# Two buffers for the attention's output weight, and the last query tile's output products moved into the next group's order

## The reference

```python
x = x + 0.5 * _L0_ffn_ref(_layernorm(x), ...)      # attention and a mixture of experts
x = x + _L0_attn_ref(_layernorm(x), ...)           # a recurrent-style token mix
x = x + 0.5 * _L0_ffn_ref(_layernorm(x), ...)      # the first part again, same weights
```

```python
q = (x @ wq).reshape(b, s, H, HD); k = (x @ wk)...; v = (x @ wv)...
q = apply_rope(q, cos, sin); k = apply_rope(k, cos, sin)
scores = jnp.einsum('bqhd,bkhd->bhqk', q, k) / np.sqrt(HD)
probs = jax.nn.softmax(jnp.where(causal, scores, min), axis=-1)
out = jnp.einsum('bhqk,bkhd->bqhd', probs, v).reshape(b, s, H * HD)
return out @ wo
```

## Time and profile before

| | |
|---|---|
| median of three runs | 1355.61 us |
| lowest and highest run | 1352.35 and 1356.25 us |
| the profiled execution, its own time | 1357.88 us |
| its span from first to last instruction | 1356.1 us |
| PE busy | 1174.1 us (87%) |
| DVE busy | 955.6 us (70%) |
| ACT busy | 773.1 us (57%) |
| POOL busy | 599.1 us (44%) |
| mean granted TensorE clock | 0.925 of full |
| chain that ended last, share by engine | PE 80%, DVE 11%, ACT 3%, DMA 2%, POOL 2% |

### The profile page before, as it was taken

The page is one execution under the profiler, slowest core; times in us unless marked ns, Lnnn a source line. Parts: engine busy times, 40 slices in busy tenths (PEclk is TensorE's granted clock), DMA queues, the critical chain, the costliest instruction groups (busy, mean ns, idle before and its releaser), DMA issues.

```text
span 1356.1 us, 18606 instructions
## 1 busy us (share of the span) xinstructions
PE 1174.1 (87%) x6576; PEld 976.2 (72%) x6576; DVE 955.6 (70%) x1799; ACT 773.1 (57%) x1510; POOL 599.1 (44%) x450
## 2 busy tenths in 40 slices
PE   5799999999999499963398799999999999849994
PEld 4688788788787378851277578878878878638883
DVE  6677677777787757748757667777777778757774
ACT  5666566666564167742453656656666656417772
POOL 3664575575610034521412375466476370004541
PEclk9899999999999589995789799999999989859998
DMA  4100100100000941124100200010010000193113
GB/s 126 36 0 2 35 1 1 35 1 1 1 1 1 318 159 51 51 81 144 51 1 1 66 1 1 1 36 1 1 36 1 1 1 1 40 347 103 51 52 117
DMA packets 48651, 66.29 MB, mean 49 GB/s; under 512 B 5808, under 2 KB 34352, under 8 KB 48432
## 3 DMA queue, kind: packets, MB, share of 16 engines
q1 hardware_dynamic: 42032, 50.94, 11.5%
q0 software_dynamic: 4416, 12.06, 2.9%
q10 hardware_dynamic: 2112, 2.10, 0.4%
HBM read 54.86 MB, written 10.22 MB: 48 GB/s over the span
## 4 chain that ended last, share of the span: by engine, by line
PE 80%; DVE 11%; ACT 3%; DMA 2%; POOL 2%; issue 2%; SPq 0%; DVEq 0%; POOLq 0%; ACTq 0%
PE ps L1375 21%; PE ps L1377 19%; PE ps L1376 19%; PE ps L1444 9%; PE ps L1505 6%; PE ps L1493 2%; PE ps L1432 1%; POOL probs L681 1%; DVE h L1079 1%; DMA xs<-rows_dram,token_of 1%; PE ps L1513 1%; PE ps L1476 1%; PE ps L1347 1%; DVE negmax L1058 1%; DVE mixT L1309 1%
## 5 line engine op out<-in xcount | busy, mean ns | idle before, releaser
L748 ACT ACTIVATE probs<-ps,negmax 128x128 f32<-128x128 f32 (+7 forms) x256 | 189.6, 741 | 109.2 <-DVE negmax L1058 106.9
L754 ACT ACTIVATE probsT<-ps 128x512 fp32r<-128x512 f32 x288 | 168.6, 597 | 135.6 <-PE ps L1444 133.4
L1058 DVE TENSOR_REDUCE negmax<-ps 128x1 f32<-128x128 f32 (+7 forms) x256 | 191.2, 751 | 64.0 <-PE ps L1432 62.0
L1063 DVE TENSOR_TENSOR probsT<-ps,probsT 128x512 fp32r<-128x512 f32 x288 | 195.0, 686 | 44.7 <-ACT probsT L754 42.8
L1444 PE MATMUL ps<-square,probs 128*128 128x128 f32 x1152 | 170.1, 275 | 5.9 <-DVE values L1053 5.9
L652 POOL DMA_INDIRECT xs<-rows_dram,token_of x46 | 68.5, 1489 | 214.3 <-DVE token_of L1154 181.8
L608 POOL TENSOR_TENSOR crossed<-crossed,rope 128x512 f32<-128x512 f32 x70 | 91.5, 1308 | 161.3 <-ACT crossed L735 161.3
L1079 DVE SCALAR_TENSOR_TENSOR h<-ps,rowinv,h 128x256 f32<-128x256 f32 x256 | 123.2, 481 | 48.5 <-PE ps L1377 36.1
L1444 PEld LDWEIGHTS ps<-square,probs 128*128 128x128 f32 x1152 | 134.1, 141 | 25.7 <-DVE values L1053 6.2
L1375 PE MATMUL ps<-keysT,queriesT 128*128 128x512 f32 (+3 forms) x384 | 141.2, 368 | 9.1 <-ACT probs L748 4.3
L1162 DVE TENSOR_TENSOR parts<-experts,parts 128x1024 fp32r<-128x1024 f32 x92 | 112.2, 1225 | 49.7 <-ACT parts L794 49.2
(11 more groups left out here) (229 smaller groups left out, 2897.7 us busy)
## 6 DMA issues: line engine op xcount, KB each, us to landing
experts<-in_L_ffn_w_dram SPq DMA_DIRECT2D x48, 512.0 KB, 10.5
w_in<-in_L_ffn_wq_dram SPq DMA_DIRECT2D x8, 512.0 KB, 3.9
wo_in<-in_L_ffn_wo_dram SPq DMA_DIRECT2D x8, 512.0 KB, 6.3
rows_dram<-probs ACTq DMA_DIRECT2D x4, 512.0 KB, 10.1
probs<-y_dram SPq DMA_DIRECT2D x8, 256.0 KB, 4.2
mixT<-y_dram SPq DMA_DIRECT2D x8, 256.0 KB, 4.7
probs<-in_L_attn_x_dram SPq DMA_DIRECT2D x2, 512.0 KB, 4.5
w_in<-in_L_ffn_wk_dram SPq DMA_DIRECT2D x8, 128.0 KB, 4.7
```

The costliest lines, as they stand in the source:

```text
L748: act.activation(probs[:, i % 2, k, 0:w], ps[:, 2 * slot_n:2 * slot_n + 2, :].rearrange("p b n -> p (b n)")[:, 0:w], ACT.Exp, bias=negmax[ ...
L754: act.activation(probsT[:, m % 3, 0, :], ps[:, 4 + m % 2, :], ACT.Copy).then_inc(S["probsT_high"], 1)
L1058: dve.tensor_reduce(negmax[:, m:m + 1], ps[:, s:s + 2, :].rearrange("p b n -> p (b n)")[:, 0:w], AX.X, ALU.max, negate=True).then_inc(S["m ...
L1063: dve.tensor_tensor(probsT[:, m % 3, 1, :], ps[:, 4 + m % 2, :], probsT[:, m % 3, 0, :].bitcast(F32), ALU.subtract).then_inc(S["probsT_low ...
```

## The change

The buffer `w_o` becomes a pair, used by even and odd groups. The second one takes the place in memory of `w_v`, the split value weight, which is needed only while the values of a call are computed. POOL now splits the next group's output weight at the end of a group's own list without waiting for that group's `out` steps: it waits for the group before it (or, in the first group, for the last value product).

The four kinds of step that project a tile out (`attn_high`, `attn_low`, `out`, `added`) go into a helper, `project_out`. A group that has a successor no longer calls it for its tile 7. The successor's order calls it for a tile -1, before anything else, and plans it among its own first steps. Two limits come with it: `values` 1,0, which needs the PSUM bank, comes after `added` -1,1, and so does `max` 3,0.

```diff
+    def project_out(i):
+        add("ACT", ("attn_high", i, 0), 0.52, i + 1.2, ("values", i, i), ("attn_high", i - 1, 0), ("out", i - 2, 1))
+        add("DVE", ("attn_low", i, 0), 0.75, i + 1.2, ("attn_high", i, 0), ("attn_low", i - 1, 0))
+        for k in range(2):
+            add("PE", ("out", i, k), 0.64, i + 1.3 + 0.2 * k, ("attn_low", i, 0), ("added", i, k - 1), ("out", i - 1, 1),
+                ("wo_split", 0, 0))
+            add("DVE", ("added", i, k), 0.95 if more or not k else 1.4, i + 1.3 + 0.2 * k, ("out", i, k), ("added", i, k - 1), ("added", i - 1, 1))
+    if carry:
+        project_out(-1)
+        later += [(("values", i, 0), ("added", -1, 1)) for i in (1,)] + [(("max", 3, 0), ("added", -1, 1))]
...
+        if i < NT - 1 or not more:
+            project_out(i)
...
+            w_o = [sb("w_o_even", [P, 2, REP, D], F32R, c=phase), None]
+            with ExitStack() as opening_phase:
+                w_v = sb("w_v", [P, 2, DC, KVH * HD], F32R, c=opening_phase)
+            w_o[1] = sb("w_o_odd", [P, 2, REP, D], F32R, c=phase)
...
-        ORDERS = {more: group_order(more)[0] for more in (True, False)}
+        ORDERS = {more: group_order(more, carry=True)[0] for more in (True, False)}
...
-                    pool.wait_ge(S["out_ps"], 2 * NT * (grp.gg + 1))
-                    split(grp.gg + 1, w_o, wo_in[:], "wo_in", 16, "wo_split")
+                    if g:
+                        pool.wait_ge(S["out_ps"], 2 * NT * grp.gg)
+                    else:
+                        pool.wait_ge(S["v_done_ps"], NT * (f + 1))
+                    split(grp.gg + 1, w_o[(grp.gg + 1) % 2], wo_in[:], "wo_in", 16, "wo_split")
...
-                        if k == 0:
-                            if i >= 2:
-                                pe.wait_ge(S["out_added"], REP * (NT * gg + i - 1))
+                        if k == 0 and (g or i >= 2):
+                            pe.wait_ge(S["out_added"], REP * (NT * gg + i - 1))
...
-                                            parts(w_o, hd, every), True, True)
+                                            parts(w_o[(gg - (i < 0)) % 2], hd, every), True, True)
```

More of the change, by code:

```diff
@@ L51, in turns_before, with group_order @@
     return i * (i + 1) // 2
-def group_order(more, opening=False):
+def group_order(more, opening=False, carry=False):
     steps = {}
@@ L99, in group_order @@
             add("PE", ("values", i, j), 0.64, at + 1.0 / (i + 1), ("low", i, j), ("values", *last), ("added", i - 2, 1))
-        add("ACT", ("attn_high", i, 0), 0.52, i + 1.2, ("values", i, i), ("attn_high", i - 1, 0), ("out", i - 2, 1))
-        add("DVE", ("attn_low", i, 0), 0.75, i + 1.2, ("attn_high", i, 0), ("attn_low", i - 1, 0))
-        for k in range(2):
-            add("PE", ("out", i, k), 0.64, i + 1.3 + 0.2 * k, ("attn_low", i, 0), ("added", i, k - 1), ("out", i - 1, 1),
-                ("wo_split", 0, 0))
-            add("DVE", ("added", i, k), 0.95 if more or not k else 1.4, i + 1.3 + 0.2 * k, ("out", i, k), ("added", i, k - 1), ("added", i - 1, 1))
+        if i < NT - 1 or not more:
+            project_out(i)
     for n, (w, k, at) in enumerate(blocks):
@@ L701, in rwkv @@
                 first_weights(1)
-                split(KVH, w_o, wo_in[:], "wo_in", 16, "wo_split")
+                split(KVH, w_o[0], wo_in[:], "wo_in", 16, "wo_split")
             attention(0)
@@ L1078, in group @@
                                 dve.wait_ge(S["out_added"], REP * (NT * gg + i) + hd)
-                            dve.scalar_tensor_tensor(out=h[:, i, :], in0=ps[:, 6 + i % 2, (hd % 2) * D:(hd % 2 + 1) * D],
-                                                     scalar=rowinv[:, m + hd:m + hd + 1], in1=h[:, i, :],
+                            dve.scalar_tensor_tensor(out=h[:, i % NT, :], in0=ps[:, 6 + i % 2, (hd % 2) * D:(hd % 2 + 1) * D],
+                                                     scalar=rowinv[:, m + hd:m + hd + 1], in1=h[:, i % NT, :],
                                                      op0=ALU.mult, op1=ALU.add).then_inc(S["out_added"], 1)
-                        if k == 1 and order is ORDERS[False]:
+                        if k == 1 and order is ORDERS[False] and i >= 0:
                             dve.wait_ge(S["out_added"], REP * (NT * gg + i + 1))
```

7 lines of the change are left out of this document (3 added, 4 removed).

## The result

The two medians differ by 2.55 us; the ratio says 0.16% less, 2.2 us, with an interval of 1.1 to 3.3 us. 1352.7 us had been predicted. Two later executions of the kernel before, at 5435 and 2407 us, lay far above all others and are left out of every median.

A forecast was written before the change was run, and what follows sets the result against it. PE's waits at six group ends were taken as what can be won. Terms -16.2 - 2.8 + 15.0 + 1.1 = -2.9 us, on the median of 1355.61 us, gave 1352.7 us; 8-in-10 range 1345 to 1361 us.

The forecast's parts named there:

- What bounds: PE's waits at six group ends, 2.33 us by brackets in the third group, can be won; POOL's late split costs nothing.
- What goes, 2.7 us a group end: At six group ends, PE's waits for `attn_low` and `added` of tile 7 disappear: 16.2 us less.
- The walk: New order queued through each later group's start: waits of 2.5, 1.8 and 3.2 us by group, 15.0 us in all.
- runs on through the slots: Behind `values` 1,0, DVE's delay from `added` -1,1 was said to cause waits before `scores` 3,2, 4,0 and 4,1.
- The mis-sized step: the last group: Each call's last group: new waits of 3.2 us, partly from squares standing behind `added` 0,1 and 1,1.
- new planning: Later in each last group, where DVE is busy for 9.16 of 10 us: 0.5 us added.
- The changes of kind: On PE, `scores` or `turn` followed by another kind of product at 22 more places, 0.05 us each: 1.1 us more.
- The clock: Before the second call's last group, TensorE's fall from 2.4 to 1.2 GHz was expected to go: 2.8 us less.
- The sum: Whole kernel: -16.2 - 2.8 + 15.0 + 1.1 = -2.9 us, or 0.2% less; 1352.7 us on the median.
- A: At group starts, the engines' room absorbs half of the new waits: 7.5 us less, 1345 us; chance 0.20.
- B: DVE bounds group starts: 8.1 us more, 1361 us; decides if new waits exceed 2.7 + 0.5 us on average; chance 0.17.
- C: At group ends, no clock fall is saved, or new pauses bring one: 2.8 us worse, 1355.5 us; chance 0.13.

The follow-up runs named there:

- e1: Kernel before with only the two output-weight buffers and POOL's earlier split, no step moved on PE, DVE or ACT: 1353.79 us, ratio 1.0001.
- e5: Changed kernel with the carried additions done on 8 of 256 columns only, so results are incomplete: 1347.07 us, ratio 0.9945.
- e6: Changed kernel with score slots exchanged in groups 2 to 4, plus `out` -1,1 ahead of `scores` 2,2 and `added` -1,1 ahead of `low` 1,1: 1348.12 us.
- e7: From e6, in second and third groups `out` 1,1 moved behind `values` 2,1 and `added` 1,1 ahead of `attn_low` 2,0: 1351.40 us, ratio 0.9982.
- e9: From e6, in second and third groups ACT does `exp` 3,1 ahead of `crossed` q1,3: 1348.14 us, ratio 0.9955.
- the first set of before: 50 timed executions of the unchanged kernel before with mean granted clock 0.923 to 0.928: median 1355.7 us.
- the second set: 40 timed executions of the unchanged kernel before with mean granted clock 0.930 to 0.933: median 1351.3 us.
- e10 b: Kernel before, unchanged, second of three single executions traced for the clock: 1356.22 us, mean clock 0.925.
- e10 c: Kernel before, unchanged, third of three single executions traced for the clock: 1356.99 us, mean clock 0.926.
- e2: Kernel before, unchanged, run again to see falls of the granted clock: 1354.85 us in 11 executions, ratio 1.0013.
- e10 a: Kernel before, unchanged, first of three single executions traced for the clock: 1354.64 us, mean clock 0.926.
- e4: Changed kernel with the last group's squares of tiles 0 and 1 done later, beside those of tiles 5 and 6: 1351.02 us, ratio 0.9976.

## Why the prediction was right, and where not

**What bounds.** Right. The six pairs of waits at the group ends were PE's loss, and their removal is the change's gain. That POOL's late split cost nothing e1 shows as far as its group lengths and its timing (to some 2 us) reach.

**What goes, 2.7 us a group end.** Right. The first group, which gives up one pair and two products of 0.75 us, should be 4.2 us shorter and is so by 3.92 and 4.56. Over all traces its mean is 109.5 us in the twelve calls of the old order and 105.1 in the sixteen of the new, 4.4 less.

**The walk.** The rows name the place, the releaser and nearly the length of its main waits. By starts, in us:

```
                              predicted   measured in after
third group: project q1,0     0.25        0.26
             values 1,0       0.55        0.69
             scores 3,2       0.4         0.43
             scores 4,0       0.45        0.18
             scores 4,1       0.15        0.32
second group: scores 2,0      0.9         0.92 (and no pause before project q1,0)
last group:  out 1,1          0.3         0.17
             scores 3,1       0.45        0.40
             scores 3,3       0.9         0.79
             scores 4,2       0.25        0.21
```

The third group was to be 0.75 us shorter and is by 0.6; the second was to stay and did. But the reason given for the waits behind `values` 1,0, a delay of DVE that "runs on through the slots", was wrong. In e5 the carried additions take half the time, the wait before `values` 1,0 goes, and none of those after it moves. The planned order asks PE, ACT and DVE for those steps at such distances that the waits arise without any delay. The walk found them because I queued the new order row by row, not because of the cause that I named. e6, e7 and e9 say the same from the other side.

**The mis-sized step: the last group.** New waits of 3.2 us, and 1.5 us of moved products with 0.25 for changes of kind, should have made it 4.95 us longer; up to the start of PE's last product it is 3.84 longer. The 0.5 us for the new planning later in the group did not come beyond a single pause of 0.20. And I had said that PE runs without a pause inside the groups, which is not so by starts: every later group has 0.28 before `scores` 2,2, and the last one also 0.20 before `scores` 3,2 and 0.49 before `out` 2,0. These went with the new order. The last shows in the trace of before:

```profile
376.25 0.39 PE L1375 MATMUL ps<-w_o,attnT 128*128 128x256 f32 x1 [0.24 <-DVE attnT L1068]
```

That is a credit of some 1 us a last group that no term of the sum had.

**The changes of kind.** The count, 22 places, holds in the two orders. The price of 0.05 us was too low. In the third group of after, `out` -1,1 stands behind a mask product and `out` 0,0 behind another `out`. They start at 254.77 and 255.56 (their rows stand above), and their second matmuls are these:

```profile
254.97 0.28 PE L1390 MATMUL ps<-w_o_odd,attnT 128*128 128x256 f32 x1
...
255.68 0.28 PE L1390 MATMUL ps<-w_o_even,attnT 128*128 128x256 f32 x1
```

The first matmul behind the mask takes 0.20 us by starts, the other 0.12. The same 0.08 to 0.09 stands in the medians of all such steps of before and after: `values` takes 0.78 us behind a `scores` or `turn` and 0.70 behind anything else, `project` 1.47 against 1.38. So the term is 1.9 us and not 1.1.

**The clock.** Right that a fall goes with the waits, as far as eight traces against six show it; the chance and size were off. It was booked as 2.8 us in every execution, and it is 1.2 to 2.1 us in four of six. A second effect of the clock had no term: the last product of a call takes 1.65 us in every undisturbed call of the old order, and 0.97 to 1.65, on average 1.12, in the sixteen calls of the new one.

**The sum.** In calls without a fall the change saves 1.26 us in the first and 1.45 in the second (396.2 to 394.75), 2.7 us in all. Of this 0.7 us is the last product at the higher clock, and 2.0 is the order, where waits, new waits and changes of kind had been put at -0.1 together. By terms: 16.2 us of waits went, and 3.1 of pauses that the sum did not have (0.28 in each of the six later groups, and 0.69 more in each last one). The new waits of the table, with the 0.69 before `values` 1,0 in every later group and the 0.26 before `project` q1,0 also in the last, are 2.5 us in the second, 1.9 in the third and 2.5 in the last group, 13.9 in both calls instead of 15.0; the changes of kind are 1.9, and the late pause of 0.20 is there twice. This would give 3.1 us, so some 1.1 us, about 0.2 in each later group, lie in differences that I could lay to no single step.

So 1352.7 us came close to 1351.98 partly by luck. The order alone saves about 2 us more than was booked, and the clock less than its 2.8 in most executions. The base was off as well: the three runs that it rests on had a median of 1355.61 us, the 22 of the comparison 1354.53. Against the first set of before the change is worth 3.7 us, which these 2.7 and a fall of some 2 us in part of the executions would about cover; against the second set it is worth nothing (1351.98 to 1351.3). What the median says hangs on how often each set occurs, and in the 22 executions compared it said 2.55.

**The rivals.** A (the waits dissolve) fell: they are there one by one. B (DVE becomes the bound) fell: the start of a group loses 2.5 us at most, below the 3.2 from which it would decide, and halving DVE's carried work gives 0.6 us a group. C (no fall of the clock is saved) fell where a fall occurs, and holds in executions that have none.

## What to carry to other kernels

A wait at a seam between two planned orders can be filled with the seam's own leftover work, but that work stands between other steps from then on: here 16 us of waits removed came back as some 14 us of smaller ones, for DVE or for ACT. Queue the new order engine by engine with durations from the trace, and count the small pauses of the old one by starts too, since brackets leave them out. Moving a step by hand in such an order did not pay everywhere: by the medians one pair of moves gave 1.7 us, one cost 3.3, and one move gave 1.2 us in one surrounding and nothing in another. When two versions are compared at a point near a fall of the clock, compare up to the start of the last step as well as to its end.

## What the runs showed of the hardware

Falls of TensorE's clock behind pauses of about 1.2 us come and go between executions of one program and change their place: before the last group of the second call, before that of the first (e1, e10 b), before the third group (e10 c), or nowhere (e2, e10 a). Pauses of up to 0.9 us within a busy group were followed by none in eight traces. Near the end of each call the clock falls too, in all fourteen traces, and what its last product takes (0.97 to 1.65 us for the same six matmuls) depends on how far it comes ahead of that fall.

A call's opening, from PE's first product of the attention to `turn` 0,0, takes one of two lengths, 24.9 or 26.2 us (once 26.0), in traces of either order (after: 26.20 in the first call, 24.91 in the second; e10 b the same; e2: 24.92 and 26.17). This is the clock. In the second call the opening is 24.9 us in the four traces whose granted clock is back at 2.4 GHz 1.5 us or more ahead of the first `project` (after, e4, e6, e10 b), and 26.2 in the ten where it comes back 3.5 to 3.8 us behind that step's start; the step takes 1.5 us in the one case and 2.7 in the other. In the first call the same two lengths of the first `project` go with the same two lengths of the opening in all fourteen traces. There its matmuls take 0.63 or 0.39 us each, while the windows view prints 1.00 for both, so this view cannot be trusted at the very start of a trace. The same 12 us ahead of and in the second opening in windows, before and then after:

```profile
748.00:760.00 12.00, 8.45 (x28) 6.47 (x28) 6.84 (x18) 7.99 (x17) 2.94 (x2) 0.57 0.63 187
```

```profile
748.00:760.00 12.00, 8.51 (x36) 6.76 (x37) 7.67 (x16) 9.29 (x19) 4.44 (x3) 0.80 0.55 167
```

So 1.3 us of any difference between two profiled executions of this kernel, in each call, may be this alone. Outside the two calls, from `turn` 0,0 to PE's last product, the fourteen traces take 558.9 to 562.0 us, whatever the order.
